# A four-layer attention and expert kernel: attention layer 2 fed batch by batch, expert tiles listed in order of completion

## The reference

```python
x = x + _L0_xattn_ref(_layernorm(x), ctx, ...)   # windowed attention, 8 heads
x = x + _L0_ffn_ref(_layernorm(x), ...)          # 8 experts, the best one per row
x = x + _L1_xattn_ref(_layernorm(x), ctx, ...)   # 16 heads of 8, softmax without a mask
x = x + _L1_ffn_ref(_layernorm(x), ...)          # 16 experts, the best 3 per row
x = x + _L2_xattn_ref(_layernorm(x), ctx, ...)
x = x + _L2_ffn_ref(_layernorm(x), ...)          # two ternary matrices, squared ReLU
x = x + _L3_xattn_ref(_layernorm(x), ctx, ...)
x = x + _L3_ffn_ref(_layernorm(x), ...)          # table lookup, then a norm
```

## Time and profile before

| what | us |
|---|---|
| median of 3 runs | 679.29 (678.29 to 683.07) |
| span of the profiled execution | 672.9 |
| busy in that span: PE, DVE, ACT, POOL | 449.5, 342.3, 241.4, 208.9 |
| layer 1's expert slots | about 130 to 183 |
| layer 2's attention, with layer 3's routing at its end | about 204 to 265 |
| layer 3's scatters | 260 to 326 |
| layer 3's expert slots | 331 to 413 |

### The profile page before, as it was taken

The page is one execution under the profiler, slowest core; times in us unless marked ns, Lnnn a source line. Parts: engine busy times, 40 slices in busy tenths (PEclk is TensorE's granted clock), DMA queues, the critical chain, the costliest instruction groups (busy, mean ns, idle before and its releaser), DMA issues.

```text
span 672.9 us, 9715 instructions
## 1 busy us (share of the span) xinstructions
PE 449.5 (67%) x2682; PEld 359.6 (53%) x2682; DVE 342.3 (51%) x1162; ACT 241.4 (36%) x634; POOL 208.9 (31%) x267
## 2 busy tenths in 40 slices
PE   0945877699807886558399895065569999985070
PEld 0933466399704675543288884034347676764050
DVE  1343445455414686353044442245577667846846
ACT  0001100266503563202166663033245656545023
POOL 4010117200065024777200002776631225523001
PEclk9975555799956898557599999556679999987565
DMA  6399951122191000111133341111100000000002
GB/s 189 60 368 353 403 225 44 55 56 65 37 339 36 2 1 24 40 51 51 58 111 107 97 115 56 51 49 42 36 0 1 1 2 0 1 1 0 0 2 62
DMA packets 58969, 53.68 MB, mean 80 GB/s; under 512 B 11458, under 2 KB 45203, under 8 KB 58788
## 3 DMA queue, kind: packets, MB, share of 16 engines
q1 hardware_dynamic: 54820, 44.67, 20.6%
q0 software_dynamic: 4096, 8.40, 4.0%
HBM read 24.20 MB, written 28.84 MB: 79 GB/s over the span
## 4 chain that ended last, share of the span: by engine, by line
PE 44%; DVE 17%; POOL 14%; issue 8%; ACT 7%; DVEq 4%; DMA 4%; SPq 2%; ACTq 0%; POOLq 0%
PE bank L1785 7%; PE bank L1772 7%; POOL rowbuf L493 7%; PE bank L1658 6%; PE bank L1674 3%; ACT xn L1311 3%; POOL rstd L481 3%; PE bank L1663 2%; PE bank L1531 2%; PE bank L1646 2%; DVE stats L599 2%; POOL h_sb L504 2%; DMA h_sb<-rowbuf 1%; PE bank L1764 1%; DVE x L1022 1%
## 5 line engine op out<-in xcount | busy, mean ns | idle before, releaser
L1399 ACT ACTIVATE r<-bank,b 128x128 f32<-128x128 f32 x224 | 68.1, 367 | 28.7 <-PE bank L1772 28.0
L493 POOL DMA_INDIRECT rowbuf<-h_sb,slots x64 | 63.1, 985 | 33.5 <-issue 17.9
L1785 PE MATMUL bank<-wall,r 128*128 x448 | 68.5, 284 | 1.4 <-ACT r L1399 1.2
L480 POOL TENSOR_SCALAR nmr<-mv 128x4 f32<-128x4 f32 x32 | 8.0, 249 | 183.2 <-DVE veps L606 178.8
L1646 PE MATMUL bank<-ident,xn 128*128 128x128 f32 x64 | 13.6, 349 | 76.1 <-ACT xn L1311 75.8
L504 POOL DMA_INDIRECT vZ<-rowbuf,slots x40 | 38.8, 971 | 73.6 <-DMA rowbuf<-h_sb 62.3
L1785 PEld LDWEIGHTS bank<-wall,r 128*128 128x128 f32 x448 | 57.3, 192 | 5.6 <-issue 3.0
L1772 PE MATMUL bank<-on,e_sb 128*128 128x128 f32 x352 | 53.7, 282 | 4.2 <-ACT on L1392 2.1
L1311 ACT ACTIVATE xn<-x,nmr,rstd 128x128 f32<-128x128 f32 x64 | 26.3, 482 | 72.7 <-POOL nmr L483 72.7
L1646 PEld LDWEIGHTS bank<-ident,xn 128*128 128x128 f32 x64 | 9.0, 176 | 79.4 <-ACT xn L1311 79.4
L1033 DVE TENSOR_TENSOR h_sb<-bank,b2all 128x128 f32<-128x128 f32 x88 | 25.6, 291 | 50.7 <-PE bank L1785 50.5
(11 more groups left out here) (262 smaller groups left out, 938.4 us busy)
## 6 DMA issues: line engine op xcount, KB each, us to landing
rowbuf<-zero SPq DMA_DIRECT2D x17, 1024.0 KB, 13.6
wall<-in_w SPq DMA_DIRECT2D x4, 2048.0 KB, 16.8
h_sb<-rowbuf SPq DMA_DIRECT2D x88, 64.0 KB, 1.8
rowbuf<-h_sb SPq DMA_DIRECT2D x88, 64.0 KB, 1.6
x<-in_x SPq DMA_DIRECT2D x4, 256.0 KB, 3.3
rowbuf<-h_sb,slots POOLq DMA_INDIRECT x64, 2.2
b2all<-in_L_ffn_b SPq DMA_DIRECT2D x1, 1024.0 KB, 16.7
out<-h_sb SPq DMA_DIRECT2D x4, 256.0 KB, 2.3
```

The costliest lines, as they stand in the source:

```text
L493: nc.gpsimd.indirect_dma_start(rowbuf[0:MOE[l][0] * REGION * P], bass.IndirectOffsetOnAxis(slots[:, k * T + t:k * T + t + 1], 0), tile_of( ...
L1399: i = a.activation(hT[:, (u % 2) * 512 + c * P:(u % 2) * 512 + (c + 1) * P], bank[2 + u % 2][:, c * P:(c + 1) * P], ACT.Relu, bias=b1[l][: ...
L1785: y = mm(bank[6 + u % 2][:, 0:P], hT[:, (u % 2) * 512 + c * P:(u % 2) * 512 + (c + 1) * P], wall[:, bass.ds(e * n + (WHALF + c * P), P)], ...
```

## The change

- **Layer 2 by batches.** `turn_x(2, b)` turns x itself, as soon as `add_experts(1, b)` is done. The norm's mean is taken out by centring the folded query weights over their 128 inputs, and its scale is applied as the `scale` of the exponential. The same is done for layer 3's gate: raw x is turned, multiplied with a centred gate (`gwc`), and the scale enters in `gate_weights`; only the rows that are scattered are still normed, beside the gate. Every norm has its own buffers.
- **New periods.** `period2` takes layer 3's steps in earlier: output turn and projection at period 5 of a batch instead of 6 and 7, turn of x at 6 instead of 10, gate at 7, slots at 8 instead of after 14. `prepare(4)` and `prepare(6)` stand between the last periods.
- **Tile lists.** Slots are 23 and 63. `tile_list(l, part, stage)` makes the list in three stages of small matmuls and DVE steps, in two parts: part 0 holds tiles that the first three batches fill (5 slots of layer 1, 21 of layer 3), part 1 the rest, ordered so that after 20 and 52 slots all rows of the first three batches are stored.
- **Waits.** SP begins a layer's loads when three batches are scattered, and waits for the fourth at slot 5 or 21; `gather` of batch 0 waits for the first 20 or 52 slots, that of batch 3 for all. Each of the 8 places of a tile has its own semaphore.
- **Weights.** Layer 3's transfers wait until layer 1's last gather has landed.

```diff
+                if l == 3:
+                    sp.wait_ge(s_gat[3], 16 * W * TOPK[1])
...
-                sp.wait_ge(s_es, 1 if l == 1 else 2)
-                now = tiles_of(0)
-                sp.wait_ge(s_sc_x, gather_before[l] + 16 * T * TOPK[l])
...
+                        if s == 0:
+                            sp.wait_ge(s_es, list_no(l, 0) + 1)
+                            for b in range(3):
+                                sp.wait_ge(s_sc_x[l][b], 16 * W * TOPK[l])
+                        if s == EARLY[l]:
+                            sp.wait_ge(s_es, list_no(l, 1) + 1)
+                            sp.wait_ge(s_sc_x[l][3], 16 * W * TOPK[l])
...
-                if b == 0 and part == 0:
-                    for r in range(2):
-                        pool.wait_ge(s_ys[r], 16 * GT * (tile_before[l] + SLOT_TILES[l]) // BODY)
+                if b in (0, 3) and part == 0:
+                    for u in range(PLACES):
+                        pool.wait_ge(s_ys[u], 16 * placed_by(l, u, PRIOR[l] if b == 0 else SLOT_TILES[l]))
...
+            def period2(t):
+                if t + 1 < T:
+                    max_sub(2, t + 1)
+                if t >= 2 and t % 2 == 0 and t < T + 2:
+                    normalise(2, (t - 2) // 2)
+                if t in (-1, 0, 3):
+                    b = (-1, 0, 3).index(t) + 1
+                    add_experts(1, b)
+                    stats_of(norm_no(2, b), b)
+                if t >= 5 and t % W == 1:
+                    b = (t - 5) // W
+                    add_y(2, b)
+                    stats_of(norm_no(3, b), b)
+                if t >= 7 and t % W == 3:
+                    gating(3, (t - 7) // W)
+                if t >= 8 and t % W == 0:
+                    route(3, (t - 8) // W)
...
+                    a.activation(e, e, ACT.Exp, scale=rstd[:, c:c + 1]).then_inc(s_exp, 1)
...
+                src = {2: tile_of(x, b, S), 3: tile_of(x, b, S), 7: tile_of(xn7, b, S)}.get(l, xn)
+                if l == 2:
+                    pe.wait_ge(s_gad, b + 1)
```

More of the change, by code:

```diff
@@ L514, in _ @@
                 power(n)
-            for part in range(2):
-                scatter(1, 0, part)
+            scatter(1, 0)
             power(7)
             for b in range(1, B):
-                for part in range(2):
-                    scatter(1, b, part)
+                scatter(1, b)
             for b in range(2):
@@ new lines, in _ @@
+            for t in range(-1, 17):
+                period2(t)
+            tile_list(3, 0, 0)
+            prepare(4, 0)
+            prepare(4, 1)
+            period2(17)
+            tile_list(3, 0, 1)
+            prepare(4, 2)
+            prepare(4, 3)
+            tile_list(3, 0, 2)
+            prepare(4, 4)
+            prepare(4, 5)
+            period2(19)
+            prepare(6, 0)
+            prepare(6, 1)
+            period2(20)
+            for stage in range(2, 6):
+                prepare(6, stage)
@@ L1803, in moe @@
[L1803 to L1812 removed]
+                        if l == 3 and s in (1, 4, 6):
+                            tile_list(3, 1, (1, 4, 6).index(s))
@@ L1813, in _ @@
+                hidden(NS - 1)
+                experts = experts_of(NS - 2 + LAG, 2)
+                second(NS - 2, experts[0])
+                second(NS - 1, experts[1])
+                turn_x(l + 1, 0)
+            prepare(2, 0)
+            tile_list(1, 1, 1)
+            prepare(2, 1)
+            tile_list(1, 1, 2)
+            for stage in range(2, 5):
                 prepare(2, stage)
             moe(1)
-            pe.wait_ge(s_aB, 4)
-            for t in range(-2, 14):
-                period(2, t)
@@ new lines, in _ @@
+            pe.wait_ge(s_aB, 4)
+            for t in range(-2, 17):
+                period2(t)
+            tile_list(3, 0, 0)
+            prepare(4, 0)
+            period2(17)
+            tile_list(3, 0, 1)
+            prepare(4, 1)
+            prepare(4, 2)
+            tile_list(3, 0, 2)
+            period2(18)
+            prepare(4, 3)
+            prepare(4, 4)
+            prepare(6, 0)
+            period2(20)
+            for stage in range(1, 5):
+                prepare(6, stage)
```

645 lines of the change are left out of this document (367 added, 278 removed).

## The result

| | before | after |
|---|---|---|
| median of 3 runs, us | 679.29 (678.29 to 683.07) | 660.65 (657.49 to 661.35) |
| ratio, 95% interval | | 0.9709 (0.9647 to 0.9771) |
| span of the profiled execution, us | 672.9 | 659.6 (its execution took 661.35) |
| first gather of layer 1's rows | 186.6 | 190.9 |
| first scores of layer 2 | 203.9 | 199.9 |

A forecast was written before the change was run, and what follows sets the result against it. No engine bounds the whole, each stage has another, and PE waits in three places. Layer 3's first gather comes 48.2 us earlier: 672.9 - 48.2 = 624.7 of span, plus 6.4 around it, 631 us; range 613 to 650.

The forecast's parts named there:

- last slot's end E: End of layer 1's slots: 183.4 plus 1.9 and 5.0 for the front, less 2.2 for one slot fewer, 188.1.
- E to layer 3's first scatter: Layer 2's first part: gathers, then 16.5 us a batch with 2 us of waiting for PE; first scatter at E + 45.
- from there to batch 2's: Layer 3's scatters: POOL and DVE both need 16.5 us a batch, so neither runs away; 30.3 us.
- from there to the first slot: Both preparations (22 us) and batch 3's pieces, 31.5 from batch 2's slots; first slot 294.2, bounds 286 and 300.
- first slot to first gather: Layer 3: 63 slots at 1.28 us, 2 us for the list; first gather at 367.7; 73.5 us.
- The front: Before layer 1's slots: new loads bring x 1.9 us later, list and centring steps cost 5 us, bounds 0 and 8.
- rival 3: Low clock in layer 2: PE at 1.2 GHz all along needs some 25 us more; 656 us, chance 0.09.
- This shift lasts to the end: Behind layer 3: the first gather's gain of 48.2 us stays whole, since what follows hangs on POOL's row of gathers.
- 6.4: Time around the span, in us, taken from the median of 679.29 standing above the span of 672.9.
- rival 1: POOL, not PE and DVE, sets the start of layer 3's slots: 286 instead of 294, 623 us, chance 0.25.
- rival 2: Batch 3's slots come late for layer 3's slot 21, past a margin of 5 us; 639 us, chance 0.12.
- The rule on the port of SBUF: DVE's float32 copies lock POOL out: 3 us over the tail's 12 gathers, 634; forecast took under 1 us.

The follow-up runs named there:

- e14_norm_p7: Kernel of e1_norm_mid with DVE's layer 7 steps moved from slots 20 and 22 to slot 16 and behind the last bias; 652.24 us, 0.9645 of the kernel before.
- e1b_norm_mid: Kernel of e1_norm_mid again, on another chip beside c1_changed_third; 646.52 us, 0.9458 of the kernel before.
- set 1: Runs on one chip where the kernel before took 698.56 us; c0_changed_again, e1_norm_mid and e3_before_wait are among them.
- c0_changed_again: The changed kernel, unaltered, run again as reference in set 1; 687.40 us, 0.9835 of the kernel before.
- e3_before_wait: Kernel before with only the wait of layer 3's weight transfers for layer 1's last gather added; 697.21 us, 0.9985 of the kernel before.
- e1_norm_mid: Changed kernel with layer 3's norms of batches 1 and 2 computed on POOL after six of the previous batch's twelve scatters; 686.00 us, 0.9793 of the kernel before.
- c1_changed_third: The changed kernel, unaltered, run again as reference beside e1b_norm_mid; 661.61 us, 0.9662 of the kernel before.

## Why the prediction was wrong, step by step

All times are on the clock of the profiled execution. The last column adds up, but for rounding, to the 28.8 us by which layer 3's first gather was later than forecast (396.5, 367.7). Two kinds of steps failed: in the batches the mechanism, an engine's queue that the sum left out, and in the others the clock, terms for DVE's steps and PE's registers that were missing, and the mean cost of a slot.

| step | predicted | measured | late by |
|---|---|---|---|
| last slot's end E | 188.1 | 191.5 | 3.4 |
| E to layer 3's first scatter | 45 | 52.0 | 7.0 |
| from there to batch 2's | 30.3 | 39.1 | 8.8 |
| from there to the first slot | 30.7 | 34.3 | 3.6 |
| first slot to first gather | 73.5 | 79.6 | 6.1 |

**E.** The front came 8.2 us later instead of 6.9, of which x has 1.1 instead of 1.9: close. The slot that is saved gave nothing: 23 slots took 50.9 us, 24 had taken 51.0. I sized the slot by its mean. Why the slots became longer is not shown.

**First gather and first scores.** Predicted E - 3.6 and E + 7, measured E - 0.6 and E + 8.4. I had moved the gather to slot 20 and not looked at what DVE does beside slots 20 and 22; e14_norm_p7 shows 2.4 us of the 3.0. The rest of this part held: landing without the weights 2.6 us, weights issued at 214.3 and nobody waiting for them.

**Layer 2's first part.** DVE waits 3.3 us for the first projection at 229.9, where I had allowed 2 per batch. PE's first tiles ran at the low clock. How much of the 7 us is the clock can be read from two profiles of the same kernel: from 200 to 238 it was 0.77 in the one and 0.90 in the other, and the first scatter started at 243.5 and 238.2. So about 5 of the 7 us go with the clock, that is with a part of rival 3, to which I gave 9 in 100 and which I had priced only as a whole.

**Batches.** This is the largest step and the one that failed in its mechanism. "A batch on POOL is 12 x 1.26 + 1.4 = 16.5 us, the same as DVE's, so neither runs away" counted POOL's work and not its order: the scale of batch b + 1 stands behind the scatters of batch b on POOL, and ACT, whose own queue carries the exponentials, waits for it. The sum had no term for ACT at all. With the norms between the scatters, e1b_norm_mid brings the 39.1 us to 33.6 at the scatters, where POOL's row now holds it, and to 31.3 at DVE's slots, 1.0 over the sum. A smaller slip stands in the sentence on POOL's pace: from 279.93 to 325.19 there are 36 scatters and so 35 intervals, 1.29 us in the mean; the 1.26 is right for scatters that nothing holds up, and the forecast does not hang on it.

**The preparation.** The path (PE, not POOL) was right: batch 2's last scatter starts at 296.6, 20 us ahead of the first slot. The sum of the pieces, 31.5 us from batch 2's slots, is 30.7 from its first scatter; 34.3 was measured. From DVE's slots it is 34.8 against 31.5. The sum had nothing for what lies between PE's last piece and the first slot. PE waits for no engine there; its program reads the first seven slots' experts into registers:

```profile
311.31 2.99 PE L1864 MATMUL bank<-vZ,wq 128*128 128x512 f32 x6 [0.97 <-DVE vZ L735]
316.95 0.43 PE L1893 MATMUL bank<-ident,h_sb 128*128 128x128 f32 x2 [2.66 <-issue]
```

Those 2.7 us are most of the 3.3; before, they lay under POOL's scatters. The clock moves the rest: I had taken the 22 us of both preparations from a stretch at 0.69, and the whole takes 32.2 to 37.8 us from DVE's slots as 0.73 to 0.56 is granted. My upper bound, 300 "if PE stays at 1.2 GHz there", was 6 us over the sum, about what the slowest group shows.

**Slots.** The mean of 1.28 was carried over; the trace gives 9.24 us for a chunk of 7, so 1.32. That is 2.5 us over 63 slots, a term mis-sized. The first three chunks, with the list's second part between them and a low clock in two, took 11.9, 10.3 and 9.9 us, 4.4 more than three others, where I had 2. The lead of the gather over the last bias, 9.0 us in the forecast, is 8.8 (396.5 and 405.3).

**Behind layer 3.** "This shift lasts to the end" held for 190 us: first gather 19.3 us earlier than before, layer 4's first scores 19.4, and still 19.4 at 588.8. It had shrunk to 17.0 at 616.9, over a stretch with a clock of 0.51 against 0.64. The last layer's first table matmuls of after:

```profile
625.23 2.94 PE L2072 MATMUL bank<-table,eT 64*128 64x193 f32 x8
629.00 2.94 PE L2072 MATMUL bank<-table,eT 64*128 64x193 f32 x8 [0.83 <-ACT eT L1593]
```

and of before:

```profile
642.20 1.75 PE L1921 MATMUL bank<-table,eT 64*128 64x193 f32 x8
644.78 1.78 PE L1921 MATMUL bank<-table,eT 64*128 64x193 f32 x8 [0.83 <-ACT eT L1495]
```

Two of the four such groups ran at the high clock before, none after: 2.4 us of the 3.7 that were lost behind 616.9. So the spans differ by 13.3.

**Around the span.** I added 6.4 us, the median less the span. The profiled execution of after took 661.35, 1.75 more than its span. In every run on record that has both numbers the time stands 1.75 to 1.87 us above the span. The 6.4 mixed that with the difference between one execution of before and the median, and it was wrong to carry it over.

**Rivals.** Batch 2's scatters never set the slots' start (rival 1), batch 3's slots were never waited for at slot 21 (rival 2: PE's waits in that stage are all for registers). Rival 3 is the nearest: the clock was 0.64 to 0.80 in layer 2 and after it. The rule on the port of SBUF that I weighed showed nothing in the starts of after either: the gathers beside the slots' copies start at 396.50 and 397.79, and 1.25 us apart from there.

## What to carry to other kernels

Where work is cut into batches that several in-order engines pass on, write down for each engine what stands in its queue between two batches, also for those that are nearly idle: here a norm of 1.5 us, queued on POOL behind 15 us of scatters, held up ACT's exponentials through a step of 1.7 us that the attention's tiles did not need, and two batches took 38.8 us or more instead of 32.8 or less. Measure a stage from the engine that bounds it: the scatters, paced by POOL, showed 3.6 us where PE and DVE had 1.2 left. Price a stretch that TensorE bounds at both clocks before you judge an edit by the time: the same preparation took 32.1 to 37.7 us, more than most edits here are worth. Loads of registers cost by the register, so the size of a chunk was no lever here.

## What the hardware showed that was not expected

**Signals of TensorE that come late.** On the chip of set 1 the two kernels took 19 and 27 us more. Their profiles agree with the others up to the first scatters. Then, beside POOL's scatters or gathers and in the few microseconds behind them, there are stretches in which what PE has done reaches the other engines late. PE and ACT of c0_changed_again beside the first gathers of layer 3's rows:

```profile
416.02 1.19 PE L1901 MATMUL bank<-on,e_sb 128*128 128x128 f32 x4 [3.03 <-issue]
...
422.05 0.63 ACT L1477 ACTIVATE r<-bank,b 128x128 f32<-128x128 f32 x2 [6.12 <-remote]
422.83 1.21 PE L1914 MATMUL bank<-wall,r 128*128 x4 [5.61 <-issue]
```

ACT needs only PE's four matmuls, done at 417.2, and starts 4.8 us later. From 405.3 to 428.5 ten groups of matmuls, three slots' work, took 23 us. In e3_before_wait on the same chip PE and DVE stood from 304 to 327.7, until 5.7 us behind the start of the last scatter (322.06):

```profile
302.52 2.08 PE L1738 MATMUL bank<-vZ,wq 128*128 128x512 f32 x2 [0.94 <-DVE vZ L686]
...
327.75 0.69 DVE L692 TENSOR_TENSOR vB<-bank,mask 128x512 f32<-128x512 f32 x1 [23.91 <-remote]
```

This also ate into e1_norm_mid's gain there: the projection that ended at 262.5 by its records reached DVE at 267.3. From batch 0 to batch 2 it still took 39.3 us at DVE's slots, where c0_changed_again took 44.3; a first batch 3.4 us later and a preparation 2.5 us longer took those 5 us back. In the answers on waits such a releaser ("remote") stands in each of the four profiles of set 1 and in none of the sixteen others. The cause was not found. The matmuls' ends are modelled, so it may be that PE itself stood still within a group.

**The same matmuls at different clocks.** In the twelve profiles with the same preparation the clock rose to its upper level at one of three places in the work: about 18 us in (at 291 in e1b_norm_mid), about 23 us in (at 306 in after) or about 32 us in (at 309 in c1_changed_third), each time while PE had waited for nobody longer than 1 us in the preparation. Hence the three groups of times. The changed kernel alone shows all three, 0.66 in after, 0.56 in c1_changed_third and 0.72 in c0_changed_again, and from 200 to 238 it was granted 0.77 in the first and 0.90 in the second. What decides between them was not found.
